# A kernel of eight attention blocks whose whole order of work is written out: every step put in a new order

## What is computed

```
# layer 0: 16 heads of 8; masks from the data
z  = mha(x, x, causal, keys cut at the row's length);  x1 = layernorm(x + z)
z  = mha(x1, context, keys cut at the row's length);   x2 = layernorm(x1 + z)
x  = layernorm(x2 + fc2(relu(fc1(x2))))
# layer 1: x = x + mha(layernorm(x), layernorm(kv)) @ Wo; x = x + W2(silu(W1 x))
# layer 2: x = x + mha(layernorm(x), same, causal); x = x + mha(layernorm(x), context); x = x + ffn(layernorm(x))
# layer 3, three times (4 heads of 32): enc = layernorm(mha(q, k, v, masks from sums) + q)
#          enc = leaky_relu(enc @ Wff + bff, 0.2) + enc; q = k = v = enc
```

## Time and profile before

| | |
|---|---|
| median of 3 runs | 972.04 us (971.81 to 972.45) |
| the profiled execution | 969.08 us |
| its span in the trace | 967.1 us, so some 2.0 us lie around it |
| mean granted clock of PE | 0.991 of full |
| PE busy | 891.9 us (92%) |
| DVE busy | 791.3 us (82%) |
| ACT busy | 603.8 us (62%) |
| POOL busy | 321.0 us (33%) |

### The profile page before, as it was taken

One profiled execution on the slowest core, in us unless ns is written; L12 is line 12 of the kernel. 1 busy time (PEld: TensorE's weight loads), 2 busy tenths in 40 slices (PEclk: granted clock), 3 DMA queues, 4 the chain that ended last, 5 costly groups with the idle time before them and its releaser, 6 DMA issues.

```text
span 967.1 us, 41172 instructions
## 1 busy us (share of the span) xinstructions
PE 891.9 (92%) x18598; PEld 650.9 (67%) x18598; DVE 791.3 (82%) x2202; ACT 603.8 (62%) x890; POOL 321.0 (33%) x389
## 2 busy tenths in 40 slices
PE   8799897899999999999999998889999999999996
PEld 4567665667677678666767766666767777766764
DVE  5899999987567756889898999999666786489896
ACT  6267665677777664455666676757777776445552
POOL 4023244531111113457543324534110112166552
PEclk9899999999999999999999999999999999999999
DMA  8000000000000000000000000000000000000001
GB/s 283 2 25 25 3 3 1 3 3 2 2 4 3 3 14 13 14 13 2 15 24 14 4 3 3 3 3 2 3 2 3 4 3 2 1 2 4 3 13 34
DMA packets 13729, 13.63 MB, mean 14 GB/s; under 512 B 618, under 2 KB 13171, under 8 KB 13299
## 3 DMA queue, kind: packets, MB, share of 16 engines
q1 hardware_dynamic: 13554, 11.00, 3.5%
HBM read 8.91 MB, written 2.10 MB: 11 GB/s over the span
## 4 chain that ended last, share of the span: by engine, by line
PE 43%; DVE 43%; ACT 6%; POOL 3%; issue 2%; DMA 1%; SPq 1%; POOLq 0%; DVEq 0%; ACTq 0%
DVE mx L1421 11%; PE pair L731 9%; PE pair L804 5%; PE pair L969 4%; DVE stats L1144 4%; PE pair L718 4%; PE pair L988 3%; DVE Y L1167 3%; PE pair L964 3%; PE pair L837 3%; DVE Y L1154 2%; DVE X L1299 2%; ACT PT L1065 2%; PE pair L946 2%; PE pair L1002 2%
## 5 line engine op out<-in xcount | busy, mean ns | idle before, releaser
L1065 ACT ACTIVATE PT<-pair 128x1024 f32<-128x1024 f32 x184 | 182.1, 1026 | 99.1 <-PE pair L969 71.1
L1421 DVE TENSOR_REDUCE mx<-pair 128x16 f32<-128x1024 f32 x184 | 217.6, 1215 | 31.0 <-PE pair L969 22.9
L731 PE MATMUL pair<-xf,W_all 128*128 128x512 f32 x336 | 173.4, 620 | 2.5 <-ACT xf L1031 1.6
L1449 POOL TENSOR_SCALAR ve<-mv 128x4 f32<-128x4 f32 x64 | 16.7, 261 | 444.2 <-DVE mv L1147 432.3
L969 PE MATMUL pair<-KQ 32*128 32x128 f32 (+1 forms) x3840 | 117.8, 252 | 6.0 <-ACT PT L1065 3.2
L969 PEld LDWEIGHTS pair<-KQ 32*128 32x128 f32 (+1 forms) x3840 | 106.8, 156 | 24.1 <-ACT PT L1065 4.5
L1031 ACT ACTIVATE KQ<-pair,c 128x512 f32<-128x512 f32 x160 | 100.7, 692 | 22.2 <-PE pair L731 21.7
L1031 ACT ACTIVATE KQ<-pair,cols 128x512 f32<-128x512 f32 x120 | 81.7, 693 | 41.5 <-PE pair L731 40.9
L1031 ACT ACTIVATE V<-pair 64x512 f32<-64x512 f32 x128 | 79.5, 621 | 42.9 <-PE pair L837 41.1
L988 PE MATMUL pair<-PT,V 128*32 128x64 f32 x5120 | 92.9, 222 | 3.7 <-DVE mx L1421 2.4
L988 PEld LDWEIGHTS pair<-PT,V 128*32 128x32 f32 x5120 | 77.0, 110 | 22.2 <-issue 5.5
(11 more groups left out here) (126 smaller groups left out, 1690.1 us busy)
## 6 DMA issues: line engine op xcount, KB each, us to landing
W_all<-weights SPq DMA_DIRECT2D x1, 2880.0 KB, 12.9
Xin<-x SPq DMA_DIRECT2D x8, 256.0 KB, 3.0
C<-ctx SPq DMA_DIRECT2D x8, 256.0 KB, 4.0
out<-X SPq DMA_DIRECT2D x8, 256.0 KB, 2.3
row<-rows SPq DMA_DIRECT2D x1, 1024.0 KB, 6.1
c<-const SPq DMA_DIRECT2D x1, 390.0 KB, 5.7
W_all<-weights SPq DMA_DIRECT2D x1, 192.0 KB, 3.0
c<-const SPq DMA_DIRECT2D x1, 93.0 KB, 2.0
```

The lines of the kernel that those rows point to most:

```text
L731: pe.matmul(t[:, 0:TOK], W(name), src[:], start=True, stop=True).then_inc(*banks.full(*use))
L1065: act.activation(PT[:, place, :], banks.of("B", a, s, v)[:], ACT.Exp, scale=float((D // (2 * PAIRS[a])) ** -0.5)).then_inc(*banks.drain((" ...
L1421: dve.tensor_reduce(dst, banks.of("A", a, s, v)[:].rearrange("p (u m t) -> p u m t", u=2, t=S), AX.X, ALU.max).then_inc(*banks.drain(("A", ...
```

## The change

The function bodies are the same; only `ORDER` differs (it is two lines shorter, so that L718 of before is L716 of after, and so on). It holds the same steps for each engine, in another order on all five. The banks and the slots of `PT` are dealt out anew, and the fillings stand at other places: 25 places with 56 fillings (77 records) where there were 30 places with 73 (94 records). By the change's description the order was searched for with step lengths and with the extra time of a step behind one of another form, each read per kind from a profile. The first rows of PE's part:

```diff
-        0.0.0 x@0; 0.0.1 x@1+8; 0.0.0 pq@0 pk@1; 0.0.3 x@2+5; 0.0.1 pq@3; 0.0.2 x@0; 0.0.0 first@1; 0.0.3 pv@2; 0.0.0
+        0.0.0 x@0 pk@0 pq@1 pv@2; 0.0.1 x@0; 0.0.0 first@1+1 length@3+2; 0.0.3 x@0; 0.0.0 maskrow@1; 0.0.1 pq@3; 0.0.0
...
```

More of the change, by code:

```diff
@@ L58 @@
[L58 to L72, removed]
@@ L173 @@
-        1.8.2 x1@0+8 ff@0; 1.8.3 x1@1+2 ff@0+4
+        0.0.0 x@0 pk@0 pq@1 pv@2; 0.0.1 x@0; 0.0.0 first@1+1 length@3+2; 0.0.3 x@0; 0.0.0 maskrow@1; 0.0.1 pq@3; 0.0.0
+        A0@23; 0.0.2 x@1; 0.0.3 pk@0; 0.0.2 pk@1; 0.0.1 pk@3; 0.0.3 pq@0; 0.0.2 pv@4; 0.0.1 first@3; 0.0.3 pv@0; 0.0.1
+        pv@5; 0.0.2 pq@2; 0.0.0 A1@30; 0.0.3 first@2+4; 0.0.2 first@4; 0.0.1 length@3; 0.0.2 length@0; 0.0.0
+        maxrow@1+1; 0.0.3 length@2; 0.0.2 maskrow@0; 0.0.1 maskrow@3; 0.0.0 B0@23+2; 0.0.2 A0@01; 0.0.1 A0@32 A1@01;
@@ new lines @@
+        0.0.3 maskrow@6; 0.0.0 v0@7 v1 B1@13 t0@4; 0.0.1 maxrow@5+1; 0.0.3 A0@01; 0.0.0 v2@4 v3; 0.0.2 A1@31; 0.0.1
+        B0@20; 0.0.0 t1@6; 0.0.2 maxrow@7+1; 0.0.1 B1@12 v0@6 v1; 0.0.3 A1@01; 0.0.1 v2@6 v3; 0.0.2 B0@20; 0.0.3
+        maxrow@2; 0.1.0 x1@3; 0.0.1 t0@6 t1@7; 0.1.0 kv@4 pq@3; 0.0.2 v0@2 v1; 0.1.0 pv@0 pk@1; 0.0.2 t0@2; 0.0.3
+        B0@23; 0.1.0 first@3; 0.0.3 B1@02; 0.1.0 length@2; 0.1.1 x1@3; 0.0.3 v0@6 v1 v2@2; 0.1.1 kv@3; 0.1.0
+        maskrow@7; 0.1.1 pq@0 pk@1; 0.1.0 A0@23; 0.1.1 pv@3; 0.3.0 ctx@0; 0.0.3 t0@1 v3; 0.1.0 A1@23; 0.0.2 B1@01;
@@ new lines @@
+        1.0.3 t0@6; 1.1.2 x1@4; 1.1.0 pv@5 maxrow@4; 1.1.2 pq@0; 1.1.1 first@1; 1.1.0 B0@12 B1@03; 1.1.1 length@4;
+        1.1.2 kv@5; 1.1.1 maskrow@4; 1.1.0 v0@2; 1.2.0 pk@3; 1.1.2 pv@5; 1.1.1 A0@03; 1.1.0 v1; 1.3.1 ctx@4; 1.1.2
+        pk@5; 1.1.0 v2@0 v3; 1.1.1 A1@32; 1.2.2 kv@1; 1.1.0 t1@0; 1.1.3 x1@2; 1.1.0 t0@3; 1.1.2 first@4; 1.1.3 kv@1;
+        1.5.0 ksum@2; 1.1.1 maxrow@5; 1.3.2 ctx@6; 1.1.3 pq@7; 1.1.2 length@1; 1.1.1 B0@12 B1@03; 1.1.2 maskrow@4;
+        1.1.3 pk@5; 1.1.1 v0@2 v1; 1.3.3 ctx@3; 1.1.3 pv@4; 1.1.2 A0@03; 1.1.1 t0@2 v2@3 v3; 1.1.2 A1@20; 1.1.3
@@ new lines @@
+        first@3; 1.2.0 x1@2; 1.5.3 pv@0; 1.1.3 length@1; 1.1.1 t1@2; 1.1.2 maxrow@3+3; 1.2.0 fc1@4; 1.2.1 pk@5 pv@2;
+        1.2.0 fc2@1; 1.1.3 maskrow@0; 1.1.2 B0@32; 1.2.0 pv@0; 1.1.3 A0@13; 1.2.1 x1@4; 1.1.2 v0@1 v1; 1.2.1 fc1@0;
+        1.1.3 A1@23; 1.5.2 pv@1; 1.2.1 fc2@0; 1.1.2 B1@12; 1.5.0 pv@1; 1.1.2 t0@2; 1.2.3 kv@3; 1.5.2 ksum@4; 1.5.1
+        ksum@5; 1.1.2 v2@6 v3; 1.5.1 pv@0; 1.2.2 pv@2; 1.1.3 maxrow@1; 1.5.0 maskrow@3; 1.2.0 q@6; 1.2.2 pk@7; 1.5.1
+        maskrow@4; 1.5.3 ksum@5; 1.5.2 maskrow@2; 1.1.2 t1@3; 1.1.3 B0@02; 1.2.0 pq@6; 1.1.3 B1@21 v0@7 v1; 1.2.0
```

496 lines of the change are left out of this document (246 added, 250 removed).

## The result

The new order takes 949.62 us (949.07 to 950.71, 4 runs) against 971.92 us for the old one (970.88 to 972.45, 4 runs): a ratio of 0.9773, 95% interval 0.9756 to 0.979. That is 22.3 us faster. The forecast was 963.5, with a range from 954 to 974, so the direction was right and the size was missed by 14 us, beyond the lower end of the range.

What follows compares the result with a forecast made beforehand. PE was taken to bound 193 to 532 and 677 to 919 us, DVE 48 to 193 and 532 to 677; 3.0 (forms) + 5.5 (PE waits) = 8.5 us off the median 972.04 gave 963.5 us, range 954 to 974.

Steps and rivals of the forecast that it cites:

- Part 3, DVE-bound stretches: 48 to 193 and 532 to 677 us, where DVE is hardly idle: taken as 0, bounds -5 and +4.
- the rival of collisions: POOL and DVE instructions block each other, 19.2 us in the DVE-bound stretches; could grow, making it slower, 976 us; chance 0.09.
- Part 1, forms of tile: PE-bound stretches: 33 fewer changes of form between neighbouring steps at 0.09 us each, 3.0 us; bounds 0 and 4.0.
- Part 4, fillings: PE-bound stretches: filling records fall from 13 to 6, 1.7 us at most; taken as nothing, since PE waited there anyway.
- Part 2, waits of PE: PE-bound stretches: fewer tight places cut PE's 22.0 us of idle time by 5.5 us; bounds 0 and 11.
- the check that I named: PE's idle time in the PE-bound stretches should fall from 22 to some 16; wrong if it stays at 20 or more.
- The clock: Rival: fewer fillings in the PE-bound stretches let PE's clock fall, some 1.7 us each time; even or slower, 975 us; chance 0.07.
- Ends: The two end stretches, 48 us each: both taken as 0, bounds -1 and +3 at the start, -2 and +2 at the end.
- The rival "More": Half of PE's waits go (11), form changes give 4, the DVE-bound stretches some 4: 953 us; chance 0.08.

Runs made afterwards that it cites:

- Without blocking: Old and new order, each with POOL's wide 128x512 instructions replaced by its power instruction on 128x4: 935.40 us with the old order, 921.59 with the new.

## Why the forecast was wrong in size

The forecast took 8.5 us off the profiled execution, all of it from the PE-bound stretches.

- **Part 3, DVE-bound stretches: the step that failed.** I took 0, with bounds of -5 and +4, because "DVE's instructions in the stretches are the same" and "an order cannot shorten DVE's work". It can: with the same instructions DVE's busy time in the second of them fell from 140.26 to 135.91 us, because fewer of them met a wide POOL instruction, and the stretch gave 5.7 us, beyond the bound. (The 0.9 of the first is too small to tell from chance; the two are 6.6 together.) The mechanism was in the text, as the rival of collisions, with its place and nearly its size ("a shift by 3 or 4 us either way is likelier"), but I let it speak only against the change and kept it out of the sum. Both lists of instructions were there, and with them which DVE step stands behind which `n1`: places like the one of `z` could have been counted as the places of bank use were. With 6.6 in the sum the forecast would have been 957, still 7 us off, with the measured time inside a range moved by as much.
- **Part 1, forms of tile: right.** 33 changes at the measured 0.084 us are 2.8; the forecast had 3.0. (Counted in the records of the two traces, with the form 64*128 of some small products apart, the PE-bound stretches have 388 and 348 changes, which would make 3.4.)
- **Part 4, fillings: wrong by some 1.4 us.** I took nothing for the fillings that leave the PE-bound stretches, because a wait was to cover them. The run without them shows that nine in the first of these stretches cost 2.1 us. Six of the nine are gone in the new order, an estimate of 1.4 by that price.
- **Part 2, waits of PE: near in the sum, wrong in the check that I named.** The PE-bound stretches lost 10.3 us. Less 2.8 for forms and 1.4 for fillings some 6 remain, where 5.5 were forecast. Without blocking it is 14.3, so some 10 remain, still within the bound of 11. That the sum came so near is in part luck: it is 9.3 us from one stretch and 1.0 from the other, and in the second POOL's blocking took some 4 us back, which the sum did not have. Idle time there fell only from 22.0 to 20.6, where I had asked for 16; by the sign that I gave, I would have been wrong. PE's busy time fell by 8.9 instead, of which forms and fillings explain some 5. But the waits did fall: those of the weight loads for other engines add up to 52.7 us before and 42.7 after in the first PE-bound stretch, 33.1 and 29.4 in the second. A product's modelled end can lie over such a wait, so idle time between products was the wrong thing to look at. How many of these us are in the time is not shown.
- **The clock: right for the PE-bound stretches.** It is 1.00 in both of them after and 0.99 or 1.00 in all profiled runs. That rival has no part in the gain there. In the first DVE-bound stretch the clock does differ between executions, and with it the old order's time. (It falls in the last stretch too, 0.96 in the earlier trace rows, which the forecast did not list.)
- **Ends:** 2.2 us lie in the two end stretches together, just beyond the bound of -2 for the last (48.1 to 45.8). Without blocking the last is the same for both orders to 0.3 us; more was not tried.
- **The base.** I subtracted from the median what I had worked out on one execution. For the old order the two lie 2.8 us apart, for the new one 0.3. So 3 us of the miss are not shown to be a mechanism of the change; they go with the clock of the execution that was profiled.

Together: 8.5 forecast; 1.8 more from the PE-bound stretches; 6.6 from the DVE-bound ones; 2.2 from the ends; 3 from the base: 22.1 of 22.3. The rival "More" (953 us, chance 0.08) came nearest to the number, but by other terms: it had 11 us of PE's waits in the sum and 4 from the DVE-bound stretches.

## What to carry to other kernels

In a stretch that DVE bounds, look at which SBUF-to-SBUF instructions of DVE stand beside wide POOL instructions: an order can put DVE's PSUM reads there instead, none of which was slowed here. A finer POOL instruction is no sure help: it gained some 2 us in one DVE-bound stretch, lost 3 in the other, and where PE waits for POOL's result it cost more than it gave. Take the wide instructions out once in both kernels: it tells what the order is worth from what the meeting of the two engines is worth. When a rival's mechanism has a size, count it in both instruction lists and put it into the sum with its sign, not into the chances alone.

## What the runs showed of the hardware

- POOL's 128x512 instructions cost the old order up to 35 us of 970, by blocking DVE and by their own length. A power instruction of POOL on 128x4 lasts nearly as long (1.01 us) and did not slow the DVE instructions beside it (1.14 us for the four of `z`).
- Beside those wide instructions DVE instructions that read PSUM kept their length (none of 736 is 0.1 us over its median), while 45 of 173 that read SBUF alone were slowed before, by up to 1.1 us for those on 128x128.
- Cutting a POOL instruction of 128x512 into four of 128x128 raises its sum from 1.29 to 1.95 us (L1473 of before, 488 ns a quarter).
- A change of tile form costs PE 0.10 us each way (320 changes, between transposes and a small product).
- The old order's executions spread over 964 to 973 us and go with PE's granted clock (0.996 to 0.984); the new order's spread over 948 to 951.
